# The second half's copies of the filter's high parts: from DMA to ScalarE

## What is computed

```python
def _layer(x, style, w, b, mw, mb, typ):
    s = style @ mw.T + mb
    weight = SCALE * w * s[:, None, :, None]
    demod = lax.rsqrt(jnp.sum(weight * weight, axis=(2, 3)) + EPS)
    weight = weight * demod[:, :, None, None]
    # 'same': conv; 'upsample': transposed conv, then blur; 'downsample': blur, then strided conv
...
x = x + _L0_cond_ref(x, cond_512, ...)   # the same for L1, L2, L3
```

## Time and profile before

| | us |
|---|---|
| median of 3 runs | 1335.65 (1335.02 to 1335.79) |
| profiled execution | 1336.1 |
| its span | 1334.3, mean granted TensorE clock 0.991 |
| PE, DVE, ACT, POOL busy | 1301.2, 1150.0, 842.1, 347.3 |

### The profile page before, as it was taken

One profiled execution on the slowest core, in us unless ns is written; L12 is line 12 of the kernel. 1 busy time (PEld: TensorE's weight loads), 2 busy tenths in 40 slices (PEclk: granted clock), 3 DMA queues, 4 the chain that ended last, 5 costly groups with the idle time before them and its releaser, 6 DMA issues.

```text
span 1334.3 us, 20141 instructions
## 1 busy us (share of the span) xinstructions
PE 1301.2 (98%) x6565; PEld 1077.7 (81%) x6565; DVE 1150.0 (86%) x1855; ACT 842.1 (63%) x1528; POOL 347.3 (26%) x632
## 2 busy tenths in 40 slices
PE   7799999999999999999999999999999999999998
PEld 5588878888888788888888778888888878888887
DVE  6798879998988899989889789989888788898885
ACT  5656466656564666666655566566566667877774
POOL 3214221133122221124131221121522233323221
PEclk7899999999999999999999999999999999999999
DMA  9235655546554465454556445565554257655643
GB/s 312 77 100 163 166 146 125 159 149 186 170 149 113 135 186 170 141 172 121 162 172 171 140 112 158 164 178 162 164 146 124 93 121 190 186 170 146 177 121 99
DMA packets 95368, 203.38 MB, mean 152 GB/s; under 512 B 10720, under 2 KB 12256, under 8 KB 95264
## 3 DMA queue, kind: packets, MB, share of 16 engines
q1 hardware_dynamic: 94896, 201.81, 52.7%
q10 hardware_dynamic: 368, 0.28, 0.1%
HBM read 72.39 MB, written 67.24 MB: 105 GB/s over the span
## 4 chain that ended last, share of the span: by engine, by line
PE 75%; DVE 15%; ACT 4%; issue 3%; POOL 2%; DMA 1%; SPq 0%; ACTq 0%; DVEq 0%; POOLq 0%
PE ps L463 74%; ACT kp L750 2%; DVE gl L1067 2%; DVE gf L1031 2%; DVE zl L980 2%; DVE xl L974 2%; DVE X L989 1%; DVE vf L1010 1%; DVE gf L1037 1%; ACT xh L709 1%; DVE vl L1017 1%; DVE vh L1019 1%; POOL w3q L1279 1%; DVE v L1015 0%; DVE gf L1043 0%
## 5 line engine op out<-in xcount | busy, mean ns | idle before, releaser
L463 PE MATMUL ps<-zh,gh 128*128 128x512 f32 (+1 forms) x1028 | 411.1, 400 | 16.2 <-DVE zl L980 12.2
L463 PE MATMUL ps<-zl,gh 128*128 128x512 f32 (+1 forms) x1028 | 407.5, 396 | 0.0
L721 ACT ACTIVATE zh<-ps,t_bx 128x512 fp32r<-128x512 f32 x256 | 175.7, 686 | 271.4 <-PE ps L463 267.9
L463 PE MATMUL ps<-zh,gl 128*128 128x512 f32 (+1 forms) x1028 | 283.0, 396 | 0.0
L750 ACT ACTIVATE kp<-ps,t_T1s 64x256 f32<-64x256 f32 x512 | 213.5, 465 | 102.8 <-PE ps L463 99.5
L463 PEld LDWEIGHTS ps<-zh,gh 128*128 128x128 f32 x1028 | 195.0, 190 | 70.0 <-DVE zl L980 20.7
L989 DVE SCALAR_TENSOR_TENSOR X<-ps,t_D,X 128x512 f32<-128x512 f32 x255 | 190.0, 745 | 61.9 <-PE ps L463 35.4
L974 DVE SCALAR_TENSOR_TENSOR xl<-X,t_S,xh 128x513 fp32r<-128x513 f32 x256 | 202.1, 809 | 35.0 <-ACT xh L709 32.8
L980 DVE SCALAR_TENSOR_TENSOR zl<-ps,t_bx,zh 128x512 fp32r<-128x512 f32 x256 | 190.7, 745 | 48.1 <-ACT zh L721 45.2
L463 PEld LDWEIGHTS ps<-zl,gh 128*128 128x128 f32 x1028 | 195.4, 190 | 44.6
L463 PEld LDWEIGHTS ps<-zh,gl 128*128 128x128 f32 x1028 | 194.7, 189 | 45.4
(11 more groups left out here) (204 smaller groups left out, 1541.3 us busy)
## 6 DMA issues: line engine op xcount, KB each, us to landing
out_x<-X SPq DMA_DIRECT2D x255, 256.5 KB, 4.9
X<-out_x SPq DMA_DIRECT2D x96, 513.0 KB, 7.0
gh<-gh SPq DMA_DIRECT2D x127, 240.0 KB, 3.0
gl<-gl SPq DMA_DIRECT2D x127, 240.0 KB, 3.6
X<-x_in SPq DMA_DIRECT2D x32, 513.0 KB, 7.6
pk<-taps_in SPq DMA_DIRECT2D x3, 512.0 KB, 12.0
pk<-pack_in SPq DMA_DIRECT2D x3, 352.0 KB, 11.2
pk<-sets_in SPq DMA_DIRECT2D x4, 256.0 KB, 8.4
```

The source lines that it names most:

```text
L463: return pe.matmul(out_ap, a, b, start=first, stop=last, skip_group_check=True)
L721: act.activation(zh[n % 2][:, ZPAD:ZPAD + M], ps[:, ZP + n % 2, :], IDENT, bias=tab["bx"][:, k, b:b + 1]).then_inc(s["zhi"], 1)
```

## The change

PE now waits for the semaphore "ghx". SP's `spread` copies gl alone. ACT copies gh by a new function `gh_cross`, one instruction a pair: it reads the half that ACT wrote and writes the other. In the loop both pairs of a quad are copied in the iteration three behind kev, ahead of the setup stages and xb; pair 1 of quad 0 is copied behind ghi_rest.

```diff
             def spread(q):
-                for name, ready, of in (("ghd", "gsh", gh), ("gld", "gsl", gl)):
-                    for h in ((2 * q, 2 * q + 1) if q else (1,)):
-                        sp.wait_ge(s[ready], h)
-                        a = flat(of[:, h % 3]).bitcast(F32)
-                        if h % 2 == 0:
-                            sp.dma_start(a[C:128, C:], a[0:C, 0:PAIR - C]).then_inc(s[name], 16)
-                        else:
-                            sp.dma_start(a[0:C, 0:PAIR - C], a[C:128, C:]).then_inc(s[name], 16)
+                for h in ((2 * q, 2 * q + 1) if q else (1,)):
+                    sp.wait_ge(s["gsl"], h)
+                    a = flat(gl[:, h % 3]).bitcast(F32)
+                    if h % 2 == 0:
+                        sp.dma_start(a[C:128, C:], a[0:C, 0:PAIR - C]).then_inc(s["gld"], 16)
+                    else:
+                        sp.dma_start(a[0:C, 0:PAIR - C], a[C:128, C:]).then_inc(s["gld"], 16)
...
                 elif i == 0 or n == 2:
-                    pe.wait_ge(s["ghd"], landed(q))
+                    pe.wait_ge(s["ghx"], 1 + 2 * q)
...
+            def gh_cross(h):
+
+                act.wait_ge(s["gsh"], h)
+                act.wait_ge(s["convg"], 2 * max(h - 2, 0))
+                halves = ((slice(0, C), slice(0, NT)), (slice(C, 128), slice(1, NT + 1)))
+                (src, of), (dst, to) = halves[h % 2], halves[1 - h % 2]
+                of, to = gh[src, h % 3, :, of, :], gh[dst, h % 3, :, to, :]
+                act.activation(to.rearrange("p i t c -> p t i c"), of.rearrange("p i t c -> p t i c").bitcast(F32), ACT.Copy) \
+                    .then_inc(s["ghx"], 1)
...
             ghi_rest()
+            gh_cross(1)
             vhi(1)
...
                 if v_at(n - 1) is not None:
                     vhi(v_at(n - 1))
+                if g_at(n - 3) is not None:
+                    q = g_at(n - 3)
+                    gh_cross(2 * q)
+                    gh_cross(2 * q + 1)
                 k, stages = setup_at(n)
```

## The result

The median is 1356.57 us (1355.62 to 1356.90, 4 runs) beside 1335.70 of the kernel before on the same chip: ratio 1.0156, 95% interval 1.0139 to 1.0174, 20.9 us slower. The forecast was 1346.1 with a range of 1339.5 to 1350.5, so the result lies outside it. The sign was right and the size was not: about half of the loss was not in the sum. The profiled execution took 1355.62 us, 19.5 above the profiled one of before; its span is 1353.7 us. What follows explains these 19.5 us; the other 1.4 lie between the profiled executions and the medians.

What follows compares the result with a forecast made beforehand. PE, busy 1301.2 of 1334.3 us, was taken to bound the kernel. 1336.1 + 5.2 (start) + 0 (blocks 0 to 2) + 5.3 (last block) = 1346.6 us, against the median 1346.1; range 1339.5 to 1350.5.

Steps and rivals of the forecast that it cites:

- The start: First quads: quad 1's late copies make convg(4) start 2.2 us later, half clock behind it costs 3.0: +5.2 us.
- The last block's ring: Last block: ACT and DVE wait on each other in turn, 20.2 us a quad against PE's 19.6: +5.3 us.
- The forecast's 0.75 us at 1121 us: Last block, at 1121.32: kev's delay left after ACT's 2.28 us wait for POOL's w3q takes part back.
- The new waits for zl: Last block, from about 1140 us: a sign, PE waiting around 0.6 us for zl at every fourth sample.
- The DMAs' absence worth nothing: Whole kernel: the 127 removed DMAs give back nothing in any engine's durations, 0 us in the sum.
- Blocks 0 to 2: The first three blocks: the copies fit in ACT's 2.50 us wait before kev, cost 0 us.
- these quads became longer than 19.6 us: Blocks 0 to 2: a sign that the prediction is wrong, if their quads become longer than 19.6 us.
- The bound "0 and 1.5 us": Blocks 0 to 2: lower and upper limit for the total cost of the copies there.
- all 45 quads together: Blocks 0 to 2: if the cover were gone, some 45 quads would lose up to 1.96 us each.
- Rival D: Last block: POOL's later w3h subtraction runs beside DVE's filter sums, another 2 to 9 us, 1348 to 1355; chance 0.1.
- gl's mere 0.23 us: DVE's gl beside POOL: stretch of 0.23 us seen in the trace, far less than a whole POOL operation.

Runs made afterwards that it cites:

- e2: The changed kernel with quad 1's two copies one iteration earlier, at the end of ACT's iteration 3: 1348.99 us, ratio 1.0097.
- e4: The changed kernel with the copies of quads 4, 17, 33 and 49 (those with the setup's squares) by DMA: 1349.34 us, ratio 1.01.
- e3: The changed kernel with the last block's copies of gh by DMA, those of blocks 0 to 2 on ACT: 1349.49 us, ratio 1.0105.
- e5: The changed kernel with only the even pairs and pair 1 copied by ACT, the other pairs by DMA: 1342.60 us, ratio 1.0055.
- e9: The changed kernel with a third ACT copy per quad in the last block, into a tile nobody reads: 1365.50 us, ratio 1.022.
- e6: The kernel before with all its DMAs, plus the same 127 ACT copies into a tile nobody reads: 1350.59 us, ratio 1.0115.
- e12: The kernel before with pair 1 and both pairs of quad 53 copied by ACT, all others by DMA: 1334.82 us, ratio 0.9975.
- e1: The kernel before with only pair 1 of gh copied by ACT, all others by DMA: 1335.04 us, ratio 0.9991.
- e11: The same kernel as e1, timed again on the same chip as e10: 1336.63 us, ratio 0.9991.
- e10: The kernel before with pair 1 and quad 1's pairs copied by ACT, the latter in iteration 3, all others by DMA: 1337.36 us, ratio 0.9997.

## Why the prediction was right and wrong

- **The start: right.** +5.2 forecast, +4.8 measured; the idle of 4.47 us at convg(4), its cause and the half clock behind it came as worked out (2.3 us for it, where the sum had 3.0), and e2 takes 5.5 us away by moving that slot alone.
- **The last block's ring: right.** Period 20.2 forecast, 20.21 measured; +5.3 forecast, 5.3 measured (e4 against e3), with each quad 0.6 us later as forecast. e5 and e9 show the threshold from both sides. The forecast's 0.75 us at 1121 us should be 0.82 (1.14 + 1.96 - 2.28), which changes little. The new waits for zl don't show as idles of 0.6 us, as the signs had it, but as a later start behind an idle of 0.07.
- **The DMAs' absence worth nothing: right** at the end of this kernel (e6), though not where PE waits for one of them at n = 212.
- **Blocks 0 to 2: wrong, and most of the miss.** The step that failed is "In the few quads in which the squares of the setup fill ACT, kev comes up to 1.96 us later, and zlo's 2.2 us just hold it. Cost: 0". kev did come 2.08 us later, and PE wasn't late in that quad by more than 0.8 us. But the sum stopped at the first product behind kev. That these quads became longer than 19.6 us is one of the signs that the prediction itself named for being wrong. The delay went on through DVE, which has no gap there, to yq, through POOL's ye and w3q to w3h in the next quad, where PE already waited for zl and has nothing in hand: its wait grew from 1.17 to 3.04 us. Three such places cost 5.4 us (after against e4), and quad 49 another 1.7 in the last block, which is most of what the last block cost above the forecast. I had read ACT's wait for w3q as cover, as at 1121.32, where it is (e12). In the edge quads that wait hangs on DVE, and so on ACT's own late kev.
- **The bound "0 and 1.5 us"** of that term was taken from zl's slack alone; the price if the cover was gone was named only for all 45 quads together. One quad's 1.96 times the four edge quads, 7.8 us, would have been the upper end, and 7.1 was measured.
- **Rival D: in part right.** POOL beside DVE cost four steps of 0.4 to 0.6 us each in blocks 0 to 2 (2.0 together; two in the filter sums, two in DVE's setup work), where I had priced it for the last block.
- **The swing of 2 us between n=202 and 208** is mostly the clock: the kernel before has its wait of 2.2 us and 3.4 us at 0.54 at n = 205, the kernel after a wait of 2.39 us and 3.4 us at 0.50 (1077.4 to 1080.8) at n = 201.
- **Open:** steps of 0.5 us at n=16 and 21 also in e4; why half a load costs blocks 0 to 2 only 1.0 us (e5); what sets how long the slow clock lasts from one execution of a kernel to the next (e1 and e11).

## What to carry over

A wait is cover for a delay only if what it waits for doesn't itself hang on the thing delayed. Follow it to its source, through the third engine and over the quad's edge, before a term is set to zero. For engines that run in a fixed order, add up the ring without its waits and compare it with the bound engine's period: above that, every turn pays, whatever the busy share. And before moving all of a set of transfers, ask which of them is ever waited for: of 127 pairs PE was seen to wait for pair 1 and for those of quad 53, and moving these three alone gave the lowest ratio (0.9975), where moving all cost 1.6%.

## What was not expected of the hardware

- **The lower clock after short waits.** In e1 PE waited 1.74 and 2.16 us, 1.6 us of work between, and then ran 4 us at 0.50. A single wait of 3.71 us brought 6.2 us of it. No run takes one of the two waits away alone; in e10 the second was 0.8 us shorter, and the clock was still 0.50 from 58 to 62 us. In e11, the same kernel as e1 with waits of 1.83 and 2.17 us, it was 0.66 there: the same waits don't always cost the same.
- **POOL beside DVE.** A 128x512 sum of DVE took 1.74 us in place of 0.69 beside a POOL operation of 1.30 us, and vl took 1.10 in place of 0.69 with POOL's w3l beside it. In the first case DVE ends at 628.32, which is 0.54 us after POOL's operation (626.48 + 1.30 = 627.78). The Trainium skill (SBUF — State Buffer, "Who interferes with whom") has the pair of ports as an exclusive lock, so that a DVE operation with two SBUF inputs waits out POOL's; here the trace agrees, with 1.05 of a possible 1.20 us. In the prediction I had put gl's mere 0.23 us against that rule: the size depends on where in POOL's operation DVE's begins, and the median of a group doesn't tell that.
- **Landing times of the same DMA.** gh's copies for quad 53 took 6.0 to 6.4 us in the execution of before, 7.3 to 7.5 in e1's and 8.1 to 9.1 in those of e10 and e11, with the engines' share near 1.0, against a median of 3.0. 0.6 us in hand in one trace was no safety.
